# Attention operands of 52 rows without cleared rows, values stored 17 wide, first stack load moved forward

## The chip, the cores and the metric

The kernel runs on one core of a Trainium2 chip (trn2). The metric is the device time of one execution in microseconds; the time of a kernel is the median of several executions. TensorE (PE, with its weight loads as PEld), VectorE (DVE), ScalarE (ACT) and GpSimd (POOL) compute; SyncE (SP) issues nearly all DMAs here, on one hardware queue that 16 DMA engines serve.

## What is computed

Two layers over x of shape (4, 1024, 256), each an attention and a mixture of experts:

```python
x = x + attn_a(layernorm(x)); x = x + ffn(layernorm(x))
x = x + attn_b(layernorm(x)); x = x + ffn(layernorm(x))
# attn_a: S = (K @ Q.T) * 16 ** -0.5 - (i - j), minus infinity where j > i; C = softmax(S); C @ V @ o_w.T + o_b
# attn_b: the usual causal attention, q @ k.T / 4, without the distance term
# 16 heads of 16 channels, T = 1024
# ffn: 2 shared experts (mean) and 32 routed ones, 6 a token by softmax weight; hidden 176, ReLU
```

## The kernel before

A loop over the layers L = 0, 1 has four stages, each closed by phase_end: every engine drains and adds to s_phase, and goes on when all five have done so.

Stage 0, projection. The 4096 tokens are 8 blocks of 512, block n = 2 b + r of batch b and half r. PE (qkv_block, L1507) forms keys, queries and values of a block in six groups; ACT copies each from PSUM with its bias to fqk or vf; DVE (qkv_block, L759) casts fqk to the high part in qkst[:, r] (L766), POOL (qk_lo) subtracts for the low part (L1383, semaphore s_pl). PE transposes the values and DVE copies them from PSUM to vst[:, r] (L776, s_vs): per block two copies of 512 elements a partition. vst is 32 wide for each head: 16 channels and ones set once a layer by a memset (L755). SP's store_block(b, r) (L398) waits for s_pl, sends four stores of 512 KB to qks_scratch (L404, s_pd[r]), waits for s_vs and sends four value stores of 256 KB in runs of 512 bytes to v_scratch (L410, s_vd[r]). DVE waits for s_pd[r] of batch b - 1 before it casts block (b, r), and for s_vd[r] before it copies its values.

The attention works on units: unit u is 4 heads of one batch, 16 units a layer. Its operands are a stack, a [128 rows, 2, 4 heads, 1024] region of SBUF for queries and keys; three stacks r = 0, 1, 2 are used in turn. Rows 0 to 47 are the channels three times over (high by high, high by low, low by high), loaded in six DMAs of 256 KB, 16 rows each (load_stack, L426). Rows 48 to 67 come from rows_scratch (load_rows, L420: two DMAs of 320 KB): zeros, the distance terms, and ones for the rows that bring in the maximum. Line 429 loads rows 66 and 67, 32 KB, after the wait for load_rows. Rows 64 to 127 are cleared first by memsets: DVE L790 and POOL L1392 for stack 0, POOL L1400 and L1407 for stacks 1 and 2. A memset may start when PE has read the xT blocks or POOL and the stores have read qkst, which lie in the same SBUF.

SP's order at the end of stage 0 is: store_block of batches 0 to 2, load_rows(0), load_stack(0, 0), store_block(3, 0), load_rows(1), load_stack(1, 1), store_block(3, 1), phase_end. Within that, load_stack(0, 0) needs the stores of batch 0. PE, after its last transposes, waits for s_vs and for stack 0 (L1722) and then runs the 38 max jobs of unit 0 (max_job, L1545): matmuls of scores into a PSUM bank, a bf16 mask matmul on the diagonal (L1556), and a DVE reduction (L801). DVE gathers the negated maxima, PE transposes them, DVE splits them (L816, L818), and PE ends the stage.

Stage 1, attention. SP waits for all stores of stage 0 (L457, L458), then load_neg_max(0) (L464) writes the negated maxima into rows 66 and 67 of the stack, then load_values(0, 0) (L433), load_rows(2), load_stack(2, 2) and the rest. PE's first_scores(0) waits for the neg-max rows. step(u) then waits for the stack of unit u + 1, whose max jobs it interleaves with the 12 slots of unit u: scores (L1566) with a bf16 mask (L1570) on the diagonal, ACT's exp (L1251), values (L1583). The stationary operand of values is 32 wide, one head for each 32 columns of PE, and the 17th column gives the denominator. Line 1722 stands in stage 0; the matmuls of L1552 and L1566 read all 128 rows of the stack.

Stage 2 runs the shared experts and the routing, stage 3 the routed experts. Neither is touched.

## Time and profile before

| | us |
|---|---|
| median of 3 runs (3132.0 to 3141.73) | 3137.55 |
| profiled execution | 3133.94 |
| its span | 3132.1 |
| granted TensorE clock, mean | 0.928 |
| PE busy, DVE busy, ACT busy, POOL busy | 2618.7, 2071.9, 1640.4, 1413.3 |
| layer 1: last value copy of stage 0 ends | 109.86 |
| layer 1: first max job; first score | 122.74; 160.49 |
| layer 2: first max job; first score | 1678.27; 1716.40 |

Times inside an execution are microseconds from the first instruction of the span. The page gives busy time and shares, the chain of work that ended last, and the costliest groups of instructions; the trace answers for single stretches, lines and DMAs. "Idle before" is what the engine waited before an instruction and for whom. SPq is the sequencer of SP, which issues the DMAs.

### The profile page before, as it was taken

What the parts mean: (1) busy time and instruction counts of PE and PEld (TensorE: products, weight loads), DVE (VectorE), ACT (ScalarE), POOL (GpSimd) and SP (SyncE); (2) the same over time, 40 slices, a digit from 0 to 9 for tenths busy, and PEclk for the clock granted to TensorE, in tenths of its full rate; (3) what the DMA queues carried; (4) which work ended last, traced back from release to release, by engine and by line L of the source; (5) the groups of instructions that cost most, each with busy time, mean ns of one, the idle gap of its engine ahead of it and who ended that gap; (6) DMA issues with size and microseconds to landing.
All of it is one profiled execution on the core that took longest, in us unless ns stands there. A gap on an engine that the chain in (4) does not pass through costs nothing.

```text
span 3132.1 us, 72446 instructions
## 1 busy us (share of the span) xinstructions
PE 2618.7 (84%) x17832; PEld 1949.9 (62%) x17832; DVE 2071.9 (66%) x4604; ACT 1640.4 (52%) x2861; POOL 1413.3 (45%) x1058
## 2 busy tenths in 40 slices
PE   7699999999882899999285999999998819999882
PEld 6455565556562888888273555555555618888882
DVE  8666676676551788777395666766775517777772
ACT  3145444544421788888341554444444208888882
POOL 3430002314155688888544200032232557888885
PEclk9899999999986999999697999999999859999996
DMA  6975655555655799888759743565457558998888
GB/s 223 231 164 124 144 100 112 146 121 165 223 192 184 158 157 154 154 153 154 172 190 208 137 84 80 100 156 117 118 157 238 201 182 147 158 157 150 151 150 204
DMA packets 317281, 494.55 MB, mean 158 GB/s; under 512 B 55706, under 2 KB 225052, under 8 KB 311772
## 3 DMA queue, kind: packets, MB, share of 16 engines
q1 hardware_dynamic: 224908, 361.85, 44.1%
q0 software_dynamic: 92160, 130.08, 24.6%
q8 instruction: 106, 1.74, 0.2%
q14 instruction: 107, 0.88, 0.1%
HBM read 264.26 MB, written 256.77 MB: 166 GB/s over the span
## 4 chain that ended last, share of the span: by engine, by line
PE 47%; DMA 16%; issue 16%; POOL 6%; DVE 6%; SPq 3%; DVEq 2%; POOLq 2%; ACT 2%; ACTq 1%
PE ps L1566 11%; PE ps L1552 11%; PE ps L1583 10%; DMA expert_sum<-x,route_u 7%; DMA expert_rows<-x 4%; PE ps L1833 4%; POOL expert_rows L1433 3%; PE ps L1570 2%; PE ps L1851 2%; POOL expert_sum L1467 2%; PE ps L1556 2%; DMA expert_rows<-work,x 2%; SPq L410 2%; PE ps L1628 1%; DMA split<-rows_scratch 1%
## 5 line engine op out<-in xcount | busy, mean ns | idle before, releaser
L1251 ACT ACTIVATE work<-ps 128x1024 f32<-128x1024 f32 (+3 forms) x768 | 594.5, 810 | 663.8 <-PE ps L1570 436.3
L1467 POOL DMA_INDIRECT expert_sum<-x,route_u x512 | 832.0, 1625 | 194.6 <-issue 102.3
L801 DVE TENSOR_REDUCE small<-ps 128x1 f32<-128x512 f32 (+3 forms) x1216 | 726.7, 655 | 211.6 <-PE ps L1556 140.1
L1433 POOL DMA_INDIRECT expert_rows<-x x288 | 284.6, 988 | 1123.5 <-DVE x L957 722.6
L1552 PE MATMUL ps<-split 128*128 128x512 f32 (+3 forms) x1536 | 511.5, 409 | 66.8 <-DVE work L829 35.3
L1566 PE MATMUL ps<-split 128*128 128x512 f32 (+3 forms) x1536 | 499.4, 405 | 28.1 <-DMA split<-split 27.1
L1833 PE MATMUL ps<-split 128*88 128x256 f32 x3072 | 418.0, 285 | 88.1 <-DVE split L1140 61.2
L1833 PEld LDWEIGHTS ps<-split 128*88 128x88 f32 x3072 | 363.9, 156 | 139.3 <-issue 138.4
L1552 PEld LDWEIGHTS ps<-split 128*128 128x128 f32 x1536 | 277.2, 201 | 262.2 <-DVE small L801 137.9
L1851 PE MATMUL ps<-split 97*128 97x256 f32 x3072 | 408.8, 282 | 2.0 <-DVE split L1155 2.0
L1851 PEld LDWEIGHTS ps<-split 97*128 97x128 f32 x3072 | 384.7, 189 | 2.4 <-issue 2.4
L1566 PEld LDWEIGHTS ps<-split 128*128 128x128 f32 x1536 | 299.0, 201 | 87.1 <-ACT work L1251 39.9
L1583 PE MATMUL ps<-work,split 128*32 128x512 f32 (+3 forms) x3072 | 329.9, 504 | 2.6 <-issue 2.6
L1821 PE MATMUL ps<-ident,x 128*128 128x128 f32 x1024 | 156.8, 276 | 115.7 <-DMA osb<-in_b1r 115.6
L1329 ACT ACTIVATE split<-split 97x512 fp32r x256 | 161.5, 631 | 162.7 <-issue 148.1
L1124 DVE CAST split<-work 128x352 fp32r x256 | 101.7, 397 | 217.0 <-issue 158.1
L1315 ACT ACTIVATE x<-ps,osb 88x256 f32<-88x256 f32 x512 | 228.8, 471 | 30.6 <-issue 15.1
L1570 PE MATMUL ps<-maskk,identb 128*128 128x128 bf16 x1024 | 233.3, 235 | 0.0
L1341 ACT ACTIVATE x<-ps,osb 128x256 f32<-128x256 f32 x512 | 212.4, 465 | 25.9 <-DMA expert_sum<-x,route_u 17.0
L1821 PEld LDWEIGHTS ps<-ident,x 128*128 128x128 f32 x1024 | 120.6, 143 | 116.7 <-issue 116.6
L1148 DVE TENSOR_TENSOR split<-split 97x512 fp32r<-97x512 f32 x256 | 176.2, 688 | 21.5 <-issue 9.2
L1556 PE MATMUL ps<-maskq,identb 128*128 128x128 bf16 (+2 forms) x704 | 187.1, 266 | 0.0
(179 smaller groups left out, 3255.6 us busy)
## 6 DMA issues: line engine op xcount, KB each, us to landing
x<-expert_rows SPq DMA_DIRECT2D x256, 320.0 KB
split<-qks_scratch SPq DMA_DIRECT2D x192, 256.0 KB
qks_scratch<-split SPq DMA_DIRECT2D x64, 512.0 KB, 4.5
expert_rows<-in_pads SPq DMA_DIRECT2D x65, 320.0 KB, 15.8
v_scratch<-work SPq DMA_DIRECT2D x64, 256.0 KB, 4.3
split<-v_scratch SPq DMA_DIRECT2D x32, 512.0 KB, 14.4
xT_scratch<-split SPq DMA_DIRECT2D x16, 1024.0 KB
split<-xT_scratch SPq DMA_DIRECT2D x16, 1024.0 KB
```

The source lines that it names most:

```text
L801: v.tensor_reduce(cols[:, heads[0]:heads[0] + len(heads), i], ps[:, task_bank(n), 0:w * len(heads)].rearrange("p (h k) -> p h k", k=w), AX ...
L1251: c.activation(pexp[:, (s % 2) * 2 + h, :, BLK - w:], ps[:, 2 * h:2 * h + 2, BLK - w:], ACT.Exp).then_inc(s_pe, 1)
L1433: pool.indirect_dma_start(rows, bass.IndirectOffsetOnAxis(ap=posu[b][:, t * 8 + k:t * 8 + k + 1], axis=0), rowb[b][:, t // TPB, t % TPB, : ...
L1467: pool.indirect_dma_start(acc[r], bass.IndirectOffsetOnAxis(ap=idx[:, j, k:k + 1], axis=0), ye[:, r3, k, :], None, compute_op=ALU.add).the ...
L1552: last = mm(bank[:, e, :], stack[:, r, 0, h, i * P:i * P + P], stack[:, r, 1, h, first:first + w], start=e == 0, stop=not diagonal and e = ...
L1556: last = mm(bank[:, :, w - P:w], identb[:, :], maskq[:, :].unsqueeze(1).broadcast_to([P, len(heads), P]), start=False, stop=True, skip_gro ...
L1566: last = mm(ps[:, h, BLK - w:], stack[:, r, 1, h, kb * P:kb * P + P], stack[:, r, 0, h, (qt + 1) * BLK - w:(qt + 1) * BLK], start=True, st ...
L1570: last = mm(ps[:, h, BLK - w:BLK - w + P], identb[:, :], maskk[:, :], start=False, stop=True, skip_group_check=True)
L1583: last = mm(ps[32 * h:32 * h + 32, 6, BLK - w:], vreg[:, r, kb, h, :], pexp[:, (s % 2) * 2 + h // 2, h % 2, BLK - w:], start=kb == 0, stop ...
L1821: last = tr(ps[:, r, k * TT + n * P:k * TT + n * P + P], xrow[:, r3, n, k * P:k * P + P], ident[:, :])
L1833: last = mm(ps[0:HC, 2 + c, 0:TT], w1e[:, r, ws, k * HID + c * HC:k * HID + c * HC + HC], xe[:, r, xp, k * TT:k * TT + TT], start=e == 0 a ...
L1851: last = mm(ps[:, 4 + 2 * (j % 2) + n, 0:D], he[0:HB, r, xp, c * TT + n * P:c * TT + n * P + P], w2e[0:HB, r3, ws, c * D:c * D + D], start ...
```

## The change

SROWS goes from 68 to 52. Rows 48 and 49 are the distance terms, 50 and 51 the maximum; no zeros are left, and the score and max matmuls read rows 0 to 51 of the stack. All memsets of stack rows go, with their waits, and load_rows waits for PE's projections instead, of blocks 0 to 3 for stack 0 and of all blocks for the others. POOL's last batch joins its loop. Values are 17 wide in SBUF and DRAM, and one DMA moves a unit's four tiles as one run of 1088 bytes a partition; DVE's copy becomes four, one for each unit. SP's loop stops a batch earlier: load_rows(0) comes ahead of batch 2's stores, load_stack(0, 0) between its two, and both stores of batch 3 ahead of load_rows(1) and load_stack(1, 1). load_neg_max(0) comes ahead of the wait for the stores.

```diff
@@ -66,7 +66,8 @@
 HG = 4
 NU = B * H // HG
 NQB = T // P
-SROWS = 68
+SROWS = 52
+VW = HD + 1
 
 NPHASE = 4
 ENGINES = 5
@@ -163,7 +164,7 @@
 
 def build(nc, a, out):
     qks = nc.dram_tensor("qks_scratch", (2, 2, NU, 64, T), F32, kind="Internal").ap()
-    vds = nc.dram_tensor("v_scratch", (NU, P, NQB, HG * 32), F32, kind="Internal").ap()
+    vds = nc.dram_tensor("v_scratch", (NU, P, 2, TPB * HG * VW), F32, kind="Internal").ap()
 
     xd = nc.dram_tensor("x_scratch", (NTOK, D), F32, kind="Internal").ap()
     xtd = nc.dram_tensor("xT_scratch", (NBLK, P, XB), F32, kind="Internal").ap()
@@ -191,7 +192,7 @@
 
         stack = split[:, 0:24576].rearrange("p (r o h t) -> p r o h t", r=3, o=2, h=HG)
         stack32 = stack.bitcast(F32)
-        vreg = split[:, 24576:27648].bitcast(F32).rearrange("p (r t h c) -> p r t h c", r=3, t=NQB, h=HG)
+        vreg = split[:, 24576:24576 + 3 * NQB * HG * VW].bitcast(F32).rearrange("p (r t h c) -> p r t h c", r=3, t=NQB, h=HG)
         wqkv = wreg[:, 0:3072].rearrange("p (m k s n) -> p m k s n", m=3, k=KD, s=2)
         qkst = wreg[:, 3072:11264].rearrange("p (r m s f t) -> p r m s f t", r=2, m=2, s=2, f=2)
         xs = split[:, 16384:20480].rearrange("p (r k s t) -> p r k s t", r=2, k=KD, s=2)
@@ -236,7 +237,7 @@
         pexp = work[:, 8192:12288].rearrange("p (r h t) -> p r h t", r=4, h=2)
         xn = work[:, 8192:10240].rearrange("p (r t d) -> p r t d", r=2, t=TPB)
         fqk = work[:, 0:2048].rearrange("p (r f t) -> p r f t", r=2, f=2)
-        vst = work[:, 2048:6144].rearrange("p (r t h c) -> p r t h c", r=2, t=TPB, h=H)
+        vst = work[:, 2048:2048 + 2 * TPB * H * VW].rearrange("p (r u t h c) -> p r u t h c", r=2, u=HG, t=TPB, h=HG)
         vf = work[:, 6144:8192].rearrange("p (r f t) -> p r f t", r=2, f=2)
         mask32 = work[:, 0:4 * P].rearrange("p (m k) -> p m k", m=4)
         rwraw = work[:, 512:576].rearrange("p (k e) -> p k e", k=KD)
@@ -300,8 +301,6 @@
         s_ph, s_pl, s_pd = sem("qk_hi_done"), sem("qk_lo_done"), [sem(f"qk_stored{r}") for r in range(2)]
         s_vt, s_vs, s_vd = sem("v_transposed"), sem("v_staged"), [sem(f"v_stored{r}") for r in range(2)]
         s_rows = [sem(f"constant_rows_loaded{r}") for r in range(3)]
-        s_zero = [sem(f"stack_zeroed{r}") for r in range(3)]
-        s_zq = sem("first_query_stack_zeroed")
         s_vl = [sem(f"values_loaded{r}") for r in range(3)]
         s_stk = [sem(f"stack_loaded{r}") for r in range(3)]
         s_st, s_pe, s_pv = sem("scoresT_ready"), sem("exp_done"), sem("values_done")
@@ -408,14 +407,13 @@
                     sp.wait_ge(s_vs, n + 1 + 1)
                     for u in range(HG):
                         sp.dma_start(
-                            vds[b * HG + u, :, r * TPB:(r + 1) * TPB, :],
-                            vst[:, r, :, HG * u:HG * u + HG, :].rearrange("p t h c -> p t (h c)")
+                            vds[b * HG + u, :, r, :],
+                            vst[:, r, u].rearrange("p t h c -> p (t h c)")
                         ).then_inc(s_vd[r], 16)
 
                 def load_rows(r):
-                    sp.wait_ge(s_zero[r], (L + 1) * (1 if r == 0 else 2))
-                    if r == 0:
-                        sp.wait_ge(s_zq, L + 1)
+                    sp.wait_ge(s_pj, (L * NBLK + (4 if r == 0 else NBLK)) * 6)
+                    apart(sp)
                     for o in range(2):
                         sp.dma_start(stack32[48:SROWS, r, o], rows_scratch[L, o].unsqueeze(1)
                                      .broadcast_to([SROWS - 48, HG, T])).then_inc(s_rows[r], 16)
@@ -426,18 +424,18 @@
                             sp.dma_start(stack32[16 * g:16 * g + 16, r, o],
                                          qks[o, s, u].rearrange("(h w) t -> w h t", h=HG)).then_inc(s_stk[r], 16)
                     sp.wait_ge(s_rows[r], (L + 1) * 32)
-                    sp.dma_start(stack32[66:68, r, 0], rows_scratch[L, 0, 0:2].unsqueeze(1)
+                    sp.dma_start(stack32[SROWS - 2:SROWS, r, 0], rows_scratch[L, 0, 2:4].unsqueeze(1)
                                  .broadcast_to([2, HG, T])).then_inc(s_stk[r], 16)
 
                 def load_values(u, r):
-                    sp.dma_start(vreg[:, r], vds[u].rearrange("p t (h c) -> p t h c", h=HG)).then_inc(s_vl[r], 16)
+                    sp.dma_start(vreg[:, r], vds[u].rearrange("p r (t h c) -> p (r t) h c", t=TPB, h=HG)).then_inc(s_vl[r], 16)
 
                 def load_unit(u, r):
                     sp.wait_ge(s_pv, (L * NU + u - 2) * NS + 2)
                     load_stack(u, r)
                     load_values(u, r)
 
-                with sp.Fori(0, B - 1) as b:
+                with sp.Fori(0, B - 2) as b:
                     for r in range(2):
                         store_block(b, r)
 
@@ -445,23 +443,22 @@
                 load_rows(0)
                 for r in range(2):
                     sp.wait_ge(s_pd[r], (L * B + 1) * 64 + 64)
+                store_block(B - 2, 0)
                 load_stack(0, 0)
-                store_block(B - 1, 0)
+                store_block(B - 2, 1)
+                for r in range(2):
+                    store_block(B - 1, r)
                 load_rows(1)
                 load_stack(1, 1)
-                store_block(B - 1, 1)
                 phase_end(sp, L, 0)
 
 
-                for r in range(2):
-                    sp.wait_ge(s_pd[r], (L * B + B) * 64 + 64)
-                    sp.wait_ge(s_vd[r], (L * B + B) * 64 + 64)
                 TASKS = L * LAYER_TASKS
 
                 def load_neg_max(u):
                     sp.wait_ge(s_mr, TASKS + max_task(u) + 1 + 3)
                     for s in range(2):
-                        sp.dma_start(stack32[66 + s:67 + s, u % 3, 0].rearrange("p h t -> p (h t)"),
+                        sp.dma_start(stack32[SROWS - 2 + s:SROWS - 1 + s, u % 3, 0].rearrange("p h t -> p (h t)"),
                                      mhl[:, s, :].bitcast(F32)).then_inc(s_mrow, 16)
 
                 def load_x_blocks(b):
@@ -497,6 +494,9 @@
                     sp.dma_start(xs[:, r].rearrange("p k s t -> p (k s t)").bitcast(F32), xtd[blk]).then_inc(s_xsl[r], 16)
 
                 load_neg_max(0)
+                for r in range(2):
+                    sp.wait_ge(s_pd[r], (L * B + B) * 64 + 64)
+                    sp.wait_ge(s_vd[r], (L * B + B) * 64 + 64)
                 load_values(0, 0)
                 load_rows(2)
                 load_stack(2, 2)
@@ -752,7 +752,7 @@
                 x_lo(0, 0)
                 x_lo(1, 1)
                 input_var(1)
-                v.memset(vst[:, :, :, :, HD:32], 1.0)
+                v.memset(vst.rearrange("p r u t h c -> p (r u t h) c")[:, :, HD:VW], 1.0)
                 input_scales(1)
                 normalise_block(2, 0)
 
@@ -772,9 +772,10 @@
                         x_lo(blk + 2, r)
                     dve.wait_ge(s_vd[r], (L * B + b) * 64 + 64)
                     dve.wait_ge(s_vt, n + 1 + 2)
-                    for f in range(2):
-                        last = v.tensor_copy(vst[:, r, :, 8 * f:8 * f + 8, 0:HD],
-                                             ps[:, 6 + f, :].rearrange("p (t h c) -> p t h c", t=TPB, h=8))
+                    for u in range(HG):
+                        last = v.tensor_copy(vst[:, r, u, :, :, 0:HD],
+                                             ps[:, 6 + u // 2, :].rearrange("p (t h c) -> p t h c", t=TPB, h=8)
+                                             [:, :, u % 2 * HG:u % 2 * HG + HG, :])
                     last.then_inc(s_vs, 1)
                     if r == 0 and b < B - 2:
                         input_var(b + 2)
@@ -786,8 +787,6 @@
                     qkv_block(B - 2, r, 3 - r)
 
 
-                dve.wait_ge(s_pj, (L * NBLK + 4) * 6)
-                v.memset(stack32[64:P, 0, 0], 0.0).then_inc(s_zq, 1)
                 for r in range(2):
                     qkv_block(B - 1, r, 1 - r)
 
@@ -1383,30 +1382,12 @@
                             p.tensor_tensor(qkst[:, r, m, 1, f], fqk[:, m, f], qkst[:, r, m, 0, f].bitcast(F32),
                                             ALU.subtract).then_inc(s_pl, 1)
 
-                with pool.Fori(0, B - 1) as b:
+                with pool.Fori(0, B) as b:
                     for r in range(2):
                         qk_lo(b, r)
-                pool.wait_ge(s_pj, (L * NBLK + 4) * 6)
-                pool.wait_ge(s_pl, (L * NBLK + 6) * 4 + 4)
-                apart(pool)
-                p.memset(stack32[64:P, 0, 1], 0.0).then_inc(s_zero[0], 1)
-                pool.wait_ge(s_zero[0], L + 1)
-                for r in range(2):
-                    qk_lo(B - 1, r)
-                pool.wait_ge(s_pj, (L + 1) * (NBLK * 6))
-                pool.wait_ge(s_pl, (L + 1) * (NBLK * 4) + 4)
-                apart(pool)
-                for o in range(2):
-                    p.memset(stack32[64:P, 1, o], 0.0).then_inc(s_zero[1], 1)
                 phase_end(pool, L, 0)
 
-                for s in range(2):
-                    pool.wait_ge(s_pd[s], (L * B + B) * 64 + 64)
-                apart(pool)
-                for o in range(2):
-                    p.memset(stack32[64:P, 2, o], 0.0).then_inc(s_zero[2], 1)
                 pool.wait_ge(s_bo, L * 16 + 16)
-                pool.wait_ge(s_zero[2], (L + 1) * 2)
                 apart(pool)
                 with pool.Fori(0, NT) as t:
                     xt = x[:, ds(t * D, D)]
@@ -1549,8 +1530,8 @@
                     diagonal = first + w == (i + 1) * P
                     task_free(n)
                     for e, h in enumerate(heads):
-                        last = mm(bank[:, e, :], stack[:, r, 0, h, i * P:i * P + P],
-                                  stack[:, r, 1, h, first:first + w], start=e == 0,
+                        last = mm(bank[:, e, :], stack[0:SROWS, r, 0, h, i * P:i * P + P],
+                                  stack[0:SROWS, r, 1, h, first:first + w], start=e == 0,
                                   stop=not diagonal and e == len(heads) - 1, skip_group_check=True)
                     if diagonal:
                         last = mm(bank[:, :, w - P:w], identb[:, :],
@@ -1563,8 +1544,8 @@
                     pe.wait_ge(s_pe, (U * NS + s) * 2 + half + 1)
                     for e in range(2):
                         h = 2 * half + e
-                        last = mm(ps[:, h, BLK - w:], stack[:, r, 1, h, kb * P:kb * P + P],
-                                  stack[:, r, 0, h, (qt + 1) * BLK - w:(qt + 1) * BLK],
+                        last = mm(ps[:, h, BLK - w:], stack[0:SROWS, r, 1, h, kb * P:kb * P + P],
+                                  stack[0:SROWS, r, 0, h, (qt + 1) * BLK - w:(qt + 1) * BLK],
                                   start=True, stop=kb < 4 * qt, skip_group_check=True)
                         if kb >= 4 * qt:
                             last = mm(ps[:, h, BLK - w:BLK - w + P], identb[:, :], maskk[:, :], start=False, stop=True,
@@ -1580,7 +1561,7 @@
                         pe.wait_ge(s_vl[r], (L * (6, 5, 5)[r] + u // 3 + 1) * 16)
                     pe.wait_ge(s_pe, (U * NS + s) * 2 + 2 + 2)
                     for h in range(HG):
-                        last = mm(ps[32 * h:32 * h + 32, 6, BLK - w:], vreg[:, r, kb, h, :],
+                        last = mm(ps[32 * h:32 * h + VW, 6, BLK - w:], vreg[:, r, kb, h, :],
                                   pexp[:, (s % 2) * 2 + h // 2, h % 2, BLK - w:], start=kb == 0,
                                   stop=kb == 4 * qt + 3, skip_group_check=True)
                     last.then_inc(s_pv, 1)
@@ -1925,9 +1906,9 @@
     r["zeros"] = np.zeros((P, D), f)
     t = np.arange(T, dtype=f)
     rows = np.zeros((NL, 2, SROWS - 48, T), f)
-    rows[0, 0, 16], rows[0, 0, 17] = -t, 1.0
-    rows[0, 1, 16], rows[0, 1, 17] = 1.0, t
-    rows[:, 1, 18:20] = 1.0
+    rows[0, 0, 0], rows[0, 0, 1] = -t, 1.0
+    rows[0, 1, 0], rows[0, 1, 1] = 1.0, t
+    rows[:, 1, 2:4] = 1.0
     r["rows"] = rows
     r["ident"] = np.eye(P, dtype=f)
     q, k = np.arange(P)[:, None], np.arange(P)[None, :]
```

## Rows read from the trace of the kernel before

**Rows 1.** The page's first lines: span, busy time and share of each engine.

```profile
span 3132.1 us, 72446 instructions
...
PE 2618.7 (84%) x17832; PEld 1949.9 (62%) x17832; DVE 2071.9 (66%) x4604; ACT 1640.4 (52%) x2861; POOL 1413.3 (45%) x1058
```

**Rows 2.** Windows of layer 1: busy us (count) per engine, PEclk, DMA share, GB/s.

```profile
108.60:122.70 14.10, 0.00 (x0) 0.00 (x0) 1.26 (x2) 0.00 (x0) 6.01 (x2) 0.54 1.02 187
...
147.80:160.50 12.70, 0.01 (x1) 0.02 (x1) 0.00 (x0) 1.28 (x1) 5.97 (x2) 0.50 0.55 186
160.50:1184.00 1023.50, 904.15 (x6016) 611.09 (x6017) 654.50 (x1484) 490.34 (x764) 344.69 (x311) 0.93 0.63 153
```

**Rows 3.** Chain that ended last, layer 1's stage change: start us, us, what.

```profile
100.96 9.88 DMA split<-rows_scratch
...
127.69 11.40 DMA split<-rows_scratch
...
151.10 6.32 DMA v_scratch<-work
157.58 0.59 SPq L464
158.22 2.13 DMA split<-split
```

**Rows 4.** Timeline, same stretch: start us, us, engine, line, tiles [idle before <-releaser].

```profile
108.57 1.29 DVE L776 COPY work<-ps 128x512 f32<-128x512 f32 x2 [3.43 <-PE ps L1527]
...
122.74 1.11 PE L1552 MATMUL ps<-split 128*128 128x128 f32 x4 [14.21 <-DMA split<-rows_scratch]
...
147.42 0.28 DVE L818 TENSOR_TENSOR split<-ps,split 32x128 fp32r<-32x128 f32 x1
...
160.49 0.79 PE L1566 MATMUL ps<-split 128*128 128x512 f32 x1 [13.42 <-DMA split<-split]
```

**Rows 5.** Line 404's stores: issued 82.5 to 84.5, then 111.2 to 113.0.

```profile
DMA to landing us min/median/max: 2.8/4.1/5.0
...
L404 SPq DMA_DIRECT2D qks_scratch<-split x4: 410/562/820, 111.2 to 113.0; - x4
...
DMA to landing us min/median/max: 10.2/12.1/14.5
```

**Rows 6.** Windows while stacks load and while stores run, columns as in group 2.

```profile
104.00:116.00 12.00, 3.68 (x20) 2.67 (x18) 2.42 (x4) 2.06 (x3) 10.10 (x5) 0.73 1.03 130
118.00:124.00 6.00, 1.26 (x6) 1.27 (x6) 0.00 (x0) 0.00 (x0) 0.00 (x0) 0.50 1.03 308
```

**Rows 7.** Timeline of DVE and POOL in the projection stage.

```profile
25.66 1.76 DVE L755 MEMSET work<- 128x2048 f32 x1 [0.38 <-issue]
...
84.64 3.59 DVE L766 CAST split<-work 128x512 fp32r<-128x512 f32 x4
...
95.63 5.49 POOL L1383 TENSOR_TENSOR split<-work,split 128x512 fp32r<-128x512 f32 x4 [1.31 <-DVE split L766]
```

**Rows 8.** Timeline of PE in unit 2: scores, mask, values.

```profile
267.39 0.23 PE L1570 MATMUL ps<-maskk,identb 128*128 128x128 bf16 x1
...
267.43 0.48 PE L1566 MATMUL ps<-split 128*128 128x512 f32 x1
...
267.75 0.23 PE L1570 MATMUL ps<-maskk,identb 128*128 128x128 bf16 x1
...
267.91 1.07 PE L1583 MATMUL ps<-work,split 128*32 128x512 f32 x8
```

**Rows 9.** The page's costliest groups: the mask matmuls.

```profile
L1570 PE MATMUL ps<-maskk,identb 128*128 128x128 bf16 x1024 | 233.3, 235 | 0.0
...
L1556 PE MATMUL ps<-maskq,identb 128*128 128x128 bf16 (+2 forms) x704 | 187.1, 266 | 0.0
```

**Rows 10.** Timeline of layer 2: first job and first score.

```profile
1678.27 1.11 PE L1552 MATMUL ps<-split 128*128 128x128 f32 x4 [13.24 <-DMA split<-rows_scratch]
...
1716.40 0.79 PE L1566 MATMUL ps<-split 128*128 128x512 f32 x1 [13.71 <-DMA split<-split]
```

## The prediction

> **What bounds the kernel now.** I read the page first: TensorE is busy 84% of the span, more than any other engine [rows 1]. Then the windows of layer 1. From 160.5 us on, through all sixteen units of the attention stage, PE is busy 904 of 1023 us at a granted clock of 0.93, while the DMA engines are busy 63% [rows 2]. There only something that makes PE itself faster or slower counts, or an earlier start of the whole stage. Between the last projection (108.6) and the first score (160.49) it is the other way round: PE and DVE stand still in 108.6 to 122.7 and again in 147.8 to 160.5, with the clock near its lower level, and in the first of the two the DMA share is 1.02 [rows 2]. The chain of waits in time says what they stand still for: the rows load of stack 0 (9.88 us), then, after PE's jobs, the rows load of stack 1 (11.40), the last value store (6.32), and the row of negated maxima (issued at 157.58, landed 2.13 us after its issue) [rows 3]. The timeline gives the two ends: PE's first max job at 122.74 is released by line 429's rows load after 14.21 us of idling, though the value copy it also needs is over at 108.57 + 1.29 = 109.86; DVE ends the maxima at 147.42 + 0.28 = 147.70; the first score starts at 160.49 [rows 4]. Layer 2 has the same two points at 1678.27 and 1716.40 [rows 10]: 38.1 us apart, 37.75 in layer 1. So I take one layer and double it.
>
> **The stack load, moved forward and made smaller.** Before, the rows load can't be issued until both memsets and every store of batch 2 have gone by, at 99.85. Now it is issued after batch 1's stores, about 79, on four partitions in place of twenty, and landed long before the stack is wanted. The six loads of stack 0 and line 429's go out behind store_block(2, 0), whose qk stores were issued up to 84.5 and landed within 5.0 us [rows 5]; its value stores follow, so the queue reaches the stack at about 90 (88 to 92). From the end of the rows load (100.96 + 9.88 = 110.84) to PE's release (122.74) the same seven loads took 11.9 us [rows 3, 4]. That gives 102, or up to 3 more where the rows load (a fifth of the bytes, half the 4 KB pieces on each of the engines that carry it) still lies ahead. The loads are slow whatever stands beside them: 130 GB/s with a DMA share of 1.03 in 104 to 116, against 308 GB/s when stores run in 118 to 124 [rows 6]. So 12 us of this queue are shifted, not saved.
>
> **What is behind them in the queue.** store_block(2, 1) is now issued at 91 behind the stack. Its qk stores hold the staging half r = 1, and DVE may not cast the last block before they have landed. Before, the stores issued behind the stack landed 10.2 to 14.5 us after issue, the last at 113.0 + 14.5 = 127.5, 4.8 us after the stack's last row [rows 4, 5]. So they land now at 102 + 4.8 = 107 (105 to 112), where DVE would have wanted them at 100.6. That is the new wait. Queued behind it on DVE are four casts (3.59 us when nothing holds them up [rows 7]) and the value copy, which releases PE. The copy is now four of 256 elements for two of 512 (1.29 us for both [rows 4]): at least 1.29, at most 2.58 if each costs what a long one does; I take 1.5. 107 + 3.6 + 1.5 = 112, plus 1 for the later landing of the value stores that the copy also waits for: the first max job starts at **113** (110 to 119) in place of 122.74.
>
> **To the first score.** The max jobs took 147.70 - 122.74 = 25.0 us, set by DVE's reductions, which don't change: 138. SP must also be through. POOL's four subtractions (5.49 us [rows 7]) end at about 113, so the last qk stores go out by 116 and the last value stores by 118; the queue works off two blocks of 2.5 MB at 308 GB/s, 8.2 us each, from 108: to 124.7. rows(1) takes up to 9.88 / 2 = 4.9 us, stack 1 another 11.9: 141.5. SP itself is past the barrier at about 132, as the wait for the rows is its last. The neg-max rows are issued at 138.3, 2.9 us ahead of a first score when the queue is empty (157.58 to 160.49 [rows 3, 4]), and behind the stack's tail otherwise. First score at **142.5** (139.5 to 150), 18 us sooner. The wait for s_pd and s_vd, which ended 9.9 us after the maxima and was ahead of the neg-max rows (157.58 against 147.70 [rows 3, 4]), now stands behind them, when both are met. load_values(0, 0) has 8 us before its first use, and moves 272 KB for 512. Stack 1 is wanted at once after the first scores and lands at 141.5: met, by a hair. If it is 5 us late, those 5 us are in the upper bound.
>
> **Small parts.** The memset of the ones writes 128 elements for 2048: some 1.6 of its 1.76 us go from DVE at 25.66 [rows 7], where DVE is never idle; of this I count 1.6 less 0.2 to 0.3 for each of the first blocks' longer value copies, 0.5 us a layer (-0.5 to 1.5). POOL's and DVE's memsets of 3.5 to 7 us lie beside PE's projections or the waits already counted: nothing more. Value stores and loads move 17/32 of the bytes in runs of 1088 for 512 bytes: nothing, as stores in the projection stage land in 2.8 to 5.0 us and are not waited for [rows 5]; during the attention stage the queue has a third of its time free. If the queue had no such room the narrower value would be a gain.
>
> **The matmuls themselves.** Scores and max jobs now have 52 rows instead of 128, at the same columns; values have 17 stationary columns for 32. No matmul of this trace has 64 rows or fewer, so this is bounded by neighbours. Below nothing: a mask is followed by values 0.16 us later, by a score 0.04 us later (267.75 to 267.91, 267.39 to 267.43 [rows 8]), so a value group carries 0.12 us that could shrink with its weights; 12 slots by 32 units are 384 groups, -46 us at the very most. Above: see the second rival. I take nought, since the moving columns stay and the score with its mask has a period of 0.36 us, 267.39 to 267.75 [rows 8], of which 640 columns at 2.4 GHz are 0.27.
>
> **The sum.** 2 x (18 + 0.5) = 37 us. The profiled execution took 3133.94 us around its span of 3132.1; 3133.9 - 37 = 3097. The median of the runs is 3.6 above it: 3100.5. Rounded **3100**, with 2 x 11 to 2 x 21 us for the bounds of this case: 3095 to 3116.
>
> **Rivals.** *Start not moved.* The stack ahead of store_block(2, 1) costs the last block all it gains: DVE's casts then end so late that the max jobs begin at 122.7 as before. Only the tail gains: 147.7 + 0.3 (my estimate for the barrier, as above) + 2.9 = 150.9 for 160.5, 19 us in two layers, 3118. For it: the stores took 14.5 us behind a stack [rows 5]; against: the queue is 10 us ahead.
>
> *Slower: the row count changes how PE is divided.* In this trace a change from the full array to 32 columns (mask to values) costs 0.12 us more than mask to score, which stay in one form [rows 8]. If 52 rows is a form of its own, every mask (1024 + 704 = 1728 of them [rows 9], 128 rows each) forces a change in and out, in a stage that PE bounds. At 0.12 each that is 207 us: 3100 + 207 = 3307. It decides from 37 / 1728 = 0.021 us a mask. Against it: there is already a gap of 0.36 - 0.27 = 0.09 us around each mask that may hide one of the two. The Trainium skill (TensorEngine Tiling (Array Packing), Key Properties) lists 64 rows by 128 columns as a tiling mode of its own and says that changing mode drains the engine; the 0.12 us at the change of columns agrees with it, and for rows no run here shows it.
>
> *Nothing changes by over 0.3%.* Another transfer, stack 1 above all, ends as late as the old chain: 3137.
>
> *PE gains too.* Half of the 46 us: 3077.
>
> **Chances.** Forecast 0.56, start not moved 0.10, change of form 0.24 (0.20 with over 0.027 us a mask, which is slower than before by over 0.3%; 0.02 within, 0.02 still faster), no change 0.04, PE gains 0.06. About 0.3%, 9.4 us, is what a measurement can tell from nothing. Faster 0.56 + 0.10 + 0.02 + 0.06 = 0.74; same 0.04 + 0.02 = 0.06; slower 0.20. The range reaches down to 3085, which leaves out most of PE's gain (0.04), and up to 3190, 0.052 us a mask (1728 x 0.052 = 90), which leaves out some 0.14.
>
> **What would show it.** First max job near 113 and first score near 142.5 in both layers; DVE's cast of the last block waiting for a qk store until 107; the seven stack loads still slow; the time from first score to the stage's end unchanged within 3 us. The prediction is wrong if a score and its mask take other than 0.36 us, if value groups take other than 1.00 us, or if PE waits for stack 1 after the first scores.

## The result, and the profile after

| | before | after |
|---|---|---|
| median, us | 3137.89 (4 runs, 3132.0 to 3141.73) | 4400.0 (4 runs, 4386.9 to 4402.18) |
| span of the profiled execution, us | 3132.1 | 4385.1 |
| granted TensorE clock, mean | 0.928 | 0.669 |
| forecast, us | | 3100 (3085 to 3190) |

The changed kernel takes 1.4016 times as long, 95% interval 1.3988 to 1.4044: 1262 us more, where 37 us less were forecast. The forecast is wrong in sign, and the change is over thirty times as large as forecast.

In the changed kernel the lines around the attention stand lower: the max jobs are L1533 (L1552 before) and their mask L1537 (L1556), the scores L1547 (L1566) and their mask L1551 (L1570), the values L1564 (L1583). The page of the changed kernel, its first lines, the row of the granted clock in 40 slices (tenths) and its groups of PE:

```profile
span 4385.1 us, 72388 instructions
...
PE 3955.8 (90%) x17832; PEld 2432.5 (55%) x17832; DVE 2130.8 (49%) x4634; ACT 1673.1 (38%) x2861; POOL 1368.4 (31%) x1048
...
PEclk9555555565555679999785555555655556799997
...
L1547 PE MATMUL ps<-split 52*128 52x512 f32 (+3 forms) x1536 | 900.0, 620 | 7.4 <-DMA split<-split 7.4
...
L1533 PE MATMUL ps<-split 52*128 52x512 f32 (+3 forms) x1536 | 826.7, 610 | 33.5 <-DVE work L828 18.8
...
L1564 PE MATMUL ps<-work,split 128*17 128x512 f32 (+3 forms) x3072 | 554.7, 820 | 0.0
...
L1551 PE MATMUL ps<-maskk,identb 128*128 128x128 bf16 x1024 | 287.9, 281 | 0.0
```

The same three groups of the kernel before:

```profile
L1552 PE MATMUL ps<-split 128*128 128x512 f32 (+3 forms) x1536 | 511.5, 409 | 66.8 <-DVE work L829 35.3
L1566 PE MATMUL ps<-split 128*128 128x512 f32 (+3 forms) x1536 | 499.4, 405 | 28.1 <-DMA split<-split 27.1
...
L1583 PE MATMUL ps<-work,split 128*32 128x512 f32 (+3 forms) x3072 | 329.9, 504 | 2.6 <-issue 2.6
```

PE waits no more than it did: its idle time ahead of these groups has shrunk (66.8 to 33.5, 28.1 to 7.4), the count of matmuls is the same 17832, and it is busy 3955.8 us against 2618.7 [rows 1]. The same instructions simply take longer. The scores went from a mean of 405 to 620 ns; the value matmuls, which stream the same columns as before, from 504 to 820 (means over all their forms). The row of the clock says where: 5 (half rate) with one 6 through both attention stages, and mostly 9 elsewhere.

Windows of the changed kernel (busy us and count for PE, PEld, DVE, ACT and POOL; granted clock, DMA share, GB/s), the columns of [rows 2], where 160.5 to 1184 had 0.93. The second ends with the last value matmul of layer 1's attention (1457.8):

```profile
170.00:1200.00 1030.00, 1022.11 (x3402) 486.17 (x3402) 388.55 (x774) 261.78 (x330) 66.07 (x69) 0.52 0.28 64
170.00:1458.00 1288.00, 1277.07 (x4307) 608.03 (x4306) 477.92 (x974) 333.90 (x422) 96.84 (x102) 0.53 0.28 67
```

The attention of layer 1 in the kernel before, whose last value matmul starts at 831.0:

```profile
170.00:831.00 661.00, 636.43 (x4313) 377.24 (x4317) 449.76 (x977) 319.32 (x423) 111.31 (x123) 0.98 0.57 139
```

The stage is nearly twice as long. From the first score to the last value matmul it takes 1457.8 - 149.97 = 1307.8 us for 831.0 - 160.49 = 670.5, and in layer 2 3646.0 - 2330.0 = 1316.0 for 2386.9 - 1716.4 = 670.5. Together these are 1283 us more, so the whole loss lies there. PE is busy 1277 of 1288 us at a granted clock of 0.53, where it was busy 636 of 661 at 0.98: it runs at the lower of its two levels (1.2 GHz) nearly all the time although the profile shows almost no idle time on it. It stays there: in 611 to 617, with PE busy without a gap, the clock is 0.50, where the kernel before has 1.00 in 612 to 617.

The timeline of PE in that stretch (start us, us, engine, line, tiles), a value group and two scores, each with its mask:

```profile
612.20 1.91 PE L1564 MATMUL ps<-work,split 128*17 128x512 f32 x8
614.04 0.79 PE L1533 MATMUL ps<-split 52*128 52x512 f32 x1
614.76 0.29 PE L1537 MATMUL ps<-maskq,identb 128*128 128x128 bf16 x1
614.98 0.79 PE L1533 MATMUL ps<-split 52*128 52x512 f32 x1
615.70 0.29 PE L1537 MATMUL ps<-maskq,identb 128*128 128x128 bf16 x1
```

A score with its mask takes 614.98 - 614.04 = 0.94 us (0.36 in [rows 8]), a value group 614.04 - 612.20 = 1.84 (1.00 before). The lower clock alone doesn't make 0.94. The kernel before also has moments at the lower level, just after its first score, and there the pair takes 161.17 - 160.49 = 0.68:

```profile
160.49 0.79 PE L1566 MATMUL ps<-split 128*128 128x512 f32 x1 [13.42 <-DMA split<-split]
161.08 0.33 PE L1570 MATMUL ps<-maskk,identb 128*128 128x128 bf16 x1
161.17 0.78 PE L1566 MATMUL ps<-split 128*128 128x512 f32 x1
```

Score to mask was 0.59 and is 0.72, mask to score was 0.09 and is 0.22: 0.13 us more at each of the two changes between 52 and 128 rows, 0.26 a pair. So there are two suspects, a lower clock and a change of form.

The stage change itself went nearly as forecast. The timeline of layer 1:

```profile
109.17 3.56 DVE L766 CAST split<-work 128x512 fp32r<-128x512 f32 x4 [10.41 <-DMA qks_scratch<-split]
112.65 1.41 DVE L776 COPY work<-ps 128x256 f32<-128x256 f32 x4
...
146.64 0.28 DVE L817 TENSOR_TENSOR split<-ps,split 32x128 fp32r<-32x128 f32 x1
```

DVE does wait for a qk store of store_block(2, 1), until 109.17 (107 forecast); the chain of waits has that store as its longest piece of this stretch, 93.12 to 109.05. The first max job starts at 114.30 (113 forecast; 122.74 in [rows 4]) and the first score at 149.97 (142.5 forecast; 160.49). Between the two the max jobs take 146.92 - 114.30 = 32.6 us instead of 25.0: here too PE is slow, with a clock of 0.52 in 108 to 150 (0.72 before) and a change of rows on both sides of each mask.

### The profile page after: what moved, and what is told of

It reads as the page before. It is cut to its first block, busy times and chain, and to the rows that moved or that the text cites. A ratio compares the mean times of both kernels' runs of the same rounds, so it can differ in the third digit from the quotient of the medians.

```text
span 4385.1 us, 72388 instructions
## 1 busy us (share of the span) xinstructions
PE 3955.8 (90%) x17832; PEld 2432.5 (55%) x17832; DVE 2130.8 (49%) x4634; ACT 1673.1 (38%) x2861; POOL 1368.4 (31%) x1048
## 4 chain that ended last, share of the span: by engine, by line
PE 66%; issue 11%; DMA 9%; POOL 4%; DVE 4%; DVEq 2%; SPq 1%; POOLq 1%; ACT 1%; ACTq 0%
PE ps L1547 18%; PE ps L1533 16%; PE ps L1564 12%; PE ps L1551 5%; PE ps L1537 4%; DMA expert_sum<-x,route_u 4%; PE ps L1814 3%; DMA expert_rows<-x 2%; PE ps L1832 2%; POOL expert_rows L1414 2%; DMA expert_rows<-work,x 2%; PE ps L1631 1%; POOL expert_sum L1448 1%; DVE split L1139 1%; PE ps L1574 1%
## 5 line engine op out<-in xcount | busy, mean ns | idle before, releaser
L1250 ACT ACTIVATE work<-ps 128x1024 f32<-128x1024 f32 (+3 forms) x768 | 621.2, 810 | 1885.4 <-PE ps L1551 1289.1
L800 DVE TENSOR_REDUCE small<-ps 128x1 f32<-128x512 f32 (+3 forms) x1216 | 783.0, 661 | 931.2 <-PE ps L1537 642.2
L1547 PE MATMUL ps<-split 52*128 52x512 f32 (+3 forms) x1536 | 900.0, 620 | 7.4 <-DMA split<-split 7.4
L1533 PE MATMUL ps<-split 52*128 52x512 f32 (+3 forms) x1536 | 826.7, 610 | 33.5 <-DVE work L828 18.8
L1533 PEld LDWEIGHTS ps<-split 52*128 52x128 f32 x1536 | 419.9, 305 | 440.4 <-issue 258.2
L1547 PEld LDWEIGHTS ps<-split 52*128 52x128 f32 x1536 | 437.4, 292 | 251.9 <-ACT work L1250 80.3
L1564 PE MATMUL ps<-work,split 128*17 128x512 f32 (+3 forms) x3072 | 554.7, 820 | 0.0
L1551 PE MATMUL ps<-maskk,identb 128*128 128x128 bf16 x1024 | 287.9, 281 | 0.0
L1551 PEld LDWEIGHTS ps<-maskk,identb 128*128 128x128 bf16 x1024 | 105.8, 103 | 285.2 <-issue 263.1
L1537 PE MATMUL ps<-maskq,identb 128*128 128x128 bf16 (+2 forms) x704 | 234.1, 332 | 0.0
L1537 PEld LDWEIGHTS ps<-maskq,identb 128*128 128x128 bf16 x704 | 73.0, 104 | 257.0 <-issue 248.6
```

What stands on the lines that cost most here:

```text
L800: v.tensor_reduce(cols[:, heads[0]:heads[0] + len(heads), i], ps[:, task_bank(n), 0:w * len(heads)].rearrange("p (h k) -> p h k", k=w), AX ...
L1250: c.activation(pexp[:, (s % 2) * 2 + h, :, BLK - w:], ps[:, 2 * h:2 * h + 2, BLK - w:], ACT.Exp).then_inc(s_pe, 1)
L1533: last = mm(bank[:, e, :], stack[0:SROWS, r, 0, h, i * P:i * P + P], stack[0:SROWS, r, 1, h, first:first + w], start=e == 0, stop=not diag ...
L1537: last = mm(bank[:, :, w - P:w], identb[:, :], maskq[:, :].unsqueeze(1).broadcast_to([P, len(heads), P]), start=False, stop=True, skip_gro ...
L1547: last = mm(ps[:, h, BLK - w:], stack[0:SROWS, r, 1, h, kb * P:kb * P + P], stack[0:SROWS, r, 0, h, (qt + 1) * BLK - w:(qt + 1) * BLK], st ...
L1551: last = mm(ps[:, h, BLK - w:BLK - w + P], identb[:, :], maskk[:, :], start=False, stop=True, skip_group_check=True)
```

## The experiments

Theory A: what counts is the number of rows that the score and max matmuls read. With fewer, the granted clock goes down, whatever the rows hold. Theory B: it is the pauses in PE at each change between 52 and 128 rows that keep the clock down. Theory C: a change of form also costs time of its own. Theory D: the narrower values, the copies or the new order of transfers have a part in it. The texts put down ahead of the first four runs use other letters for two things: "A64" is the theory that only a matmul of 64 rows or fewer is another form of the array, and "C" is the 17 columns of the values, a part of D here.

### Only fewer rows read, in the kernel before

```
-  stack[:, r, 0, h, ...], stack[:, r, 1, h, ...]
+  stack[0:SROWS, r, 0, h, ...], stack[0:SROWS, r, 1, h, ...]     # SROWS = 68, max jobs and scores
```

Rows 68 to 127 of a stack are zeros in the kernel before, so this leaves out only multiplications by zero.

> The kernel before, with one edit: its score and max matmuls read rows 0 to 67 of the stack instead of all 128 (rows 68 on are zeros, so nothing else changes). Theory A, fewer rows of the array in use, whatever their number, keep the granted clock down: slower, by 200 us and more, clock in the attention stage below 0.9. Theory A64, only a matmul of 64 rows or fewer is another form of the array: no difference, 3138 within 10 us, score and mask 0.36 us apart. Theory C, the 17 columns of the values are to blame: no difference either.

3633.04 us (3612.37 to 3652.86), ratio 1.1601 (1.1549 to 1.1653). The row of the clock, and a window of layer 1:

```profile
PEclk9679655655668799999785896665565686999996
...
170.00:1200.00 1030.00, 988.47 (x4763) 585.36 (x4763) 535.00 (x1171) 354.29 (x464) 166.60 (x180) 0.69 0.45 114
```

The clock falls to 0.69 in this stretch, from 0.94 in the same window of the kernel before, and the kernel takes 496 us more, with the same instructions, the same columns, the same loads and stores. A mask at 613 us and the max matmul behind it: 68 rows are of the same form as 128 (mask to score 0.09 us at the lower clock, as before):

```profile
613.30 0.33 PE L1556 MATMUL ps<-maskq,identb 128*128 128x128 bf16 x1
613.39 0.67 PE L1552 MATMUL ps<-split 68*128 68x384 f32 x1
```

That is theory A, with no change of form in it. A64 had forecast no difference, so a change of form can't be all of it.

### The change with 68 rows

```
-SROWS = 52
+SROWS = 68
-    rows[:, 1, 2:4] = 1.0
+    rows[:, 1, SROWS - 50:SROWS - 48] = 1.0
```

> The changed kernel with SROWS back at 68 and still no cleared rows: rows 52 to 65 are zeros loaded from DRAM, the matmuls read rows 0 to 67. Everything else of the change stays. Theory A: slow as the first run of this set, less the gain of the new order. Theory A64: clock 0.93 again, first max job at 115 to 120 (the rows loads are 320 KB again), first score at 143 to 148, 3138 less 25 to 35 us: 3103 to 3113. Theory C: still above 4000.

3625.86 us (3600.13 to 3642.59), ratio 1.1575 (1.1532 to 1.1618). The window, then a score and its mask at the upper clock:

```profile
170.00:1200.00 1030.00, 979.80 (x4745) 577.47 (x4745) 530.52 (x1166) 353.69 (x462) 169.28 (x175) 0.70 0.43 112
```

```profile
310.33 0.47 PE L1547 MATMUL ps<-split 68*128 68x512 f32 x1
310.65 0.23 PE L1551 MATMUL ps<-maskk,identb 128*128 128x128 bf16 x1
310.69 0.47 PE L1547 MATMUL ps<-split 68*128 68x512 f32 x1
```

The pair takes 0.36 us, as in [rows 8]: at the upper level, 68 rows cost nothing. A64's 3103 to 3113 fails here too. Everything else of the change is in this kernel, and it stands within the noise of the first experiment; the 36 us that this rest turns out to gain further down can't be seen beside the 40 us between the runs of either. So 488 of the 1262 us are there with 68 rows, and 774 (4400 - 3626) come with going from 68 to 52.

### Only the narrower values

```
-  ps[32 * h:32 * h + 32, 6, ...], vreg[:, r, kb, h, :]
+  ps[32 * h:32 * h + 17, 6, ...], vreg[:, r, kb, h, 0:17]      # in the kernel before
```

> The kernel before, with only the stationary operand of the value matmuls cut from 32 to 17 columns (storage unchanged). Theories A and A64: 3138 within 10 us, a value group of 512 columns still takes 1.00 us. Theory C, 17 columns of each 32 keep the clock down: above 3700, granted clock near 0.67.

3140.4 us in one run, against 3137.35 (3132.54 to 3144.31, 7 runs) for the kernel before, clock 0.93 in 170 to 1200. In that run the 17 columns neither cost nor bring anything that could be told from the spread of the kernel before.

### The masks in halves of 64 rows

The changed kernel, with each mask matmul of 128 rows split into two of 64, so that a score and its mask have the same form:

```
-  mm(..., identb[:, :], maskk[:, :], start=False, stop=True)
+  for z, (idn, msk) in enumerate(((identb[0:64, :], maskk[0:64, :]), (identh, maskkh))):
+      mm(..., idn, msk, start=False, stop=z == 1)               # the same for maskq
```

> The changed kernel, with each mask matmul of 128 rows split into two of 64 rows on the same half of the array as the scores, so that score and mask never differ in rows. 52 rows and 17 columns stay. Theory A64, clock part from the rows: the granted clock stays at 0.5 in the attention stage, score and mask period falls from 0.94 to 0.75 to 0.80 us, the whole to 4050 to 4200. Theory B, the clock is down because the changes of form leave pauses on PE: clock back at 0.9 and more, 3150 to 3300. Theory C: clock at 0.5 as well, so this run tells B from the others.

4156.41 us in one run. Its window, and one score with its two half masks:

```profile
170.00:1200.00 1030.00, 1019.32 (x4419) 572.68 (x4415) 422.93 (x846) 285.76 (x360) 92.55 (x96) 0.53 0.31 74
```

```profile
613.10 0.77 PE L1540 MATMUL ps<-split 52*128 52x512 f32 x1
613.68 0.33 PE L1545 MATMUL ps<-maskq,identb 64*128 64x128 bf16 x1
613.80 0.31 PE L1545 MATMUL ps<-halfb 64*128 64x128 bf16 x1
613.88 0.77 PE L1540 MATMUL ps<-split 52*128 52x512 f32 x1
```

With 1728 matmuls more it is 244 us faster, and both the time (4050 to 4200) and the period (0.75 to 0.80) are those forecast. The score goes over to its mask after 0.58 us, not 0.72, and the whole period is 0.78 in place of 0.94; 1728 x 0.16 = 276 us would be the gain if all were like this one. The second half mask costs 613.80 - 613.68 = 0.12, 1728 x 0.12 = 207: without it the changes of form at the masks would be worth some 244 + 207 = 450 us, against 1728 x 0.26 = 449 by the pair. But the clock stays at 0.53, with almost no pauses left at the masks. Theory B falls as the main cause, theory C holds. A small part of the pauses in the low clock isn't excluded: the masks read 64 rows here, and 0.53 is so near 0.50, the lower level, that little could show.

### All of the change, with 128 rows read

This puts back what the change removed from the operands, and keeps the rest. The stacks have 64 rows of data, rows 64 to 127 are cleared as before, and the matmuls read all 128. The order of loads and stores, the four-fold value copies and the 17-wide values are those of the change.

```
-SROWS = 52
+SROWS = 64                                  # rows[:, 1, SROWS - 50:SROWS - 48] = 1.0
+    ...                                     # semaphores s_zero, with waits on PE, VectorE and GpSimd
+    v.memset(stack32[64:P, 0, o], 0.0)      # VectorE, between the last two projection blocks
+    p.memset(stack32[64:P, 1, o], 0.0)      # GpSimd, end of stage 0; the same for stack 2, a stage later
-  stack[0:SROWS, r, ...]
+  stack[:, r, ...]                          # max jobs and scores
```

> The changed kernel with its own order of loads and stores, its 17-wide values and its four-fold value casts, but score and max matmuls that read all 128 rows, of which 64 to 127 are cleared again (operands of 64 rows, the clearing on VectorE for stack 0 and on GpSimd for stacks 1 and 2). All of the work is computed. Theory A (what was lost lies only in the number of rows the matmuls read; the earlier start of the attention is worth what was forecast): the granted clock is back at 0.93 in 170:1200, the first max job stands near 114 us and the first score near 142 to 146 us, and the time is 3100 to 3115 us against 3137 of the kernel before. Theory D (the new order of transfers or the casts cost something of their own, hidden so far beneath the slow matmuls): the clock is back but the time is 3137 or above.

3099.88 us (3094.13 to 3105.22, 5 runs) against 3135.57 (3132.51 to 3146.66, 13 runs): ratio 0.988 (0.9859 to 0.9902), 36 us faster than the kernel before, 1.2%, with an interval that leaves out nought. Theory A had forecast 3100 to 3115. Its page and window:

```profile
span 3092.3 us, 72412 instructions
...
PEclk9899999999986999999698999999999859999996
```

```profile
170.00:1200.00 1030.00, 905.41 (x6094) 618.60 (x6090) 663.43 (x1509) 505.14 (x805) 342.86 (x294) 0.94 0.62 150
```

Its timeline at the two stage changes (the max jobs are L1548 here, the scores L1562):

```profile
109.32 3.56 DVE L767 CAST split<-work 128x512 fp32r<-128x512 f32 x4 [1.92 <-DMA qks_scratch<-split]
...
112.81 1.41 DVE L777 COPY work<-ps 128x256 f32<-128x256 f32 x4
...
114.55 1.11 PE L1548 MATMUL ps<-split 128*128 128x128 f32 x4 [7.12 <-DVE work L777]
...
139.37 0.28 DVE L821 TENSOR_TENSOR split<-ps,split 32x128 fp32r<-32x128 f32 x1
...
145.23 0.79 PE L1562 MATMUL ps<-split 128*128 128x512 f32 x1 [6.22 <-DMA split<-split]
...
1677.80 0.79 PE L1562 MATMUL ps<-split 128*128 128x512 f32 x1 [4.46 <-DMA split<-split]
```

The first score is 160.49 - 145.23 = 15.3 us sooner in layer 1, and 1716.40 - 1677.80 = 38.6 sooner in layer 2 [rows 4, 10]; the span is 39.8 shorter. Theory D (the transfers or the copies cost something of their own) falls. This version beats both kernels.

### How the clock depends on the rows

The kernel before, with max jobs and scores that read `stack[0:96, ...]`, and with `stack[0:112, ...]`; the rest of the rows is zeros.

> The kernel before with score and max matmuls that read 96 of the 128 rows (the rest is zeros, so nothing of the result is left out). If the granted clock falls with the number of rows gradually, the time lies between 3137 us (128 rows, clock 0.93 in 170:1200) and 3633 us (68 rows, 0.69), around 3300 to 3450. If there is one step between 68 and 128 rows, it is equal to one of the two ends.

> The kernel before with score and max matmuls that read 112 of the 128 rows (the rest is zeros, nothing of the result is left out). With a gradual dependence the time lies between that of 96 rows and 3137 us; with a step above 112 rows it is near 3633 us; with one below 96 it is 3137 us.

96 rows: 3230.54 us (3211.78 to 3249.29), ratio 1.0295 (1.0233 to 1.0357). 112 rows: 3152.4 us (3138.91 to 3162.98), ratio 1.004 (1.0016 to 1.0065). In 170 to 1200 the clock is 0.87 and 0.93.

That window isn't the same work in every kernel. The last value matmul of layer 1 starts at 831.0 us in the kernel before, at 1080.4 in the first experiment and at 1457.8 in the changed kernel. So in the faster kernels 170 to 1200 also holds later work, stages 2 and 3 above all, which the change doesn't touch (831 to 1200 in the kernel before: clock 0.87). The attention stage alone, from 170 us to its last value matmul, for 112, 96 and 68 rows in the kernel before, then for 64 rows in the changed one (the run of the next section):

```profile
170.00:842.00 672.00, 645.49 (x4321) 382.59 (x4318) 451.61 (x977) 318.94 (x423) 110.55 (x122) 0.96 0.57 137
170.00:893.00 723.00, 697.81 (x4329) 411.31 (x4329) 455.43 (x978) 321.32 (x424) 111.14 (x123) 0.88 0.53 128
170.00:1080.00 910.00, 891.48 (x4319) 506.85 (x4318) 466.80 (x978) 327.52 (x424) 111.04 (x123) 0.66 0.42 102
170.00:1455.00 1285.00, 1274.09 (x4307) 605.57 (x4306) 477.43 (x974) 334.44 (x422) 97.21 (x102) 0.53 0.28 68
```

There is no single step between 128 and 68: 128, 112, 96 and 68 rows give a clock of 0.98, 0.96, 0.88 and 0.66 in the attention, and 3137, 3152, 3231 and 3633 us. Both forecasts of a gradual fall held in sign; 96 rows lie below the 3300 to 3450 that I had named, since the loss is small at first.

### 64 rows

The changed kernel with `SROWS = 64` (and the two ones of `rows` moved along).

> The changed kernel with operands of 64 rows in place of 52 (nothing left out). 52 and 64 rows differ from 68 in that they fit in half of the array. If the form is what counts below 68 rows, this is like 52 rows: 4300 to 4450 us, the pair of a 512-wide score and its mask at 0.94 us and a clock of 0.50 to 0.57 in 170:1200. If only the number of rows counted, it would be close to the 3626 us of 68 rows, 3650 to 3750.

4378.97 us (4373.44 to 4384.49), ratio 1.3955 (1.3911 to 1.3998). PE at 613.95:

```profile
613.95 0.79 PE L1533 MATMUL ps<-split 64*128 64x512 f32 x1
614.68 0.29 PE L1537 MATMUL ps<-maskq,identb 128*128 128x128 bf16 x1
614.90 0.79 PE L1533 MATMUL ps<-split 64*128 64x512 f32 x1
```

The pair takes 0.95 us and the clock is 0.53 in 170 to 1200. Twelve more rows than 52 bring 21 us; four more, from 64 to 68, bring 753. The change of form begins between 64 and 68 rows.

### The change of form where the clock is high

The masks in halves of 64 rows again, now in the kernel before with its 128-row scores: the form changes at each mask and back.

> The kernel before (score and max matmuls of 128 rows, values 32 wide), with each mask matmul of 128 rows split into two of 64 rows: 1728 matmuls more, and a change of form from 128 to 64 rows and back around each mask pair. Nothing is left out. It measures the change of form where the granted clock is high. Theory C (a change of form costs time of its own, 0.27 us for the two of a pair at the lower clock, so 0.13 us at the upper one): a pair of a 512-wide score and its mask takes 0.36 + 0.13 + some 0.07 for the second half, about 0.56 us, and the time is 1728 x 0.2 = some 350 us above 3137 us, 3350 to 3550, with the granted clock in 170:1200 still at 0.85 or more. Rival (a change of form costs nothing, the 0.27 us in the changed kernel came with the low clock alone): the pair takes 0.36 + 0.07 = 0.43 us, and the time is 3200 to 3280 us.

3848.7 us (3830.01 to 3867.4), ratio 1.2274 (1.213 to 1.2418). The window, then a stretch in which the clock is 1.00:

```profile
170.00:1200.00 1030.00, 1006.61 (x5208) 500.20 (x5208) 474.30 (x1003) 332.23 (x428) 121.51 (x137) 0.81 0.39 92
```

```profile
218.73 0.49 PE L1574 MATMUL ps<-split 128*128 128x512 f32 x1
219.16 0.23 PE L1579 MATMUL ps<-maskk,identb 64*128 64x128 bf16 x1
219.22 0.22 PE L1579 MATMUL ps<-halfb 64*128 64x128 bf16 x1
219.37 0.50 PE L1574 MATMUL ps<-split 128*128 128x512 f32 x1
```

The period is 0.64 us for 0.36 [rows 8]. Score to mask is 0.43 for 0.32, the second half 0.06, mask to score 0.15 for 0.04: 0.11 at each change, 0.22 a pair. So a change of form costs nearly as much at the upper clock as the 0.13 at the lower one, and I had expected half. By the pair the kernel would lose 1728 x 0.28 = 484 us; it loses 713, and the clock of the stretch is 0.81 where I had expected 0.85 or more (and 0.56 us for the pair, 3350 to 3550 for the kernel). The remaining 229 us are put down to the clock, which fell from 0.98 to 0.81 in the attention (170 to 1190 here); that is a difference, not a measurement. Whether it is the 64 rows of the masks or the pauses beside them that lower it here wasn't told apart.

## Why the prediction was wrong

**What bounds the kernel: right.** PE sets the attention stage, and only what makes PE faster or slower counts. That made the error dear: PE is busy 1337 us more (3955.8 less 2618.7), and the kernel takes 1262 us more. One reading of [rows 2] was off: 160.5 to 1184 isn't the attention stage alone, whose last value matmul starts at 831.0; the rest is later work, at a clock of 0.86. In the attention itself PE was busy 636 of 661 us at 0.98, so PE bounded it more tightly than 904 of 1023 says, and there was more clock to lose than 0.93 shows.

**The stack load and the queue behind it: right, to some 2 us.** The stack's loads go out at 88.3 in both versions (88 to 92 forecast), DVE's wait ends at 109.2 to 109.3 (107), the value copy takes 1.41 us (1.5), the first max job starts at 114.3 and 114.55 (113). The four value copies of 256 elements cost 0.12 more than the two of 512 [rows 4].

**To the first score: right with 128 rows, with one term short.** The max jobs take 139.65 - 114.55 = 25.1 us (25.0). The row of negated maxima is issued at 139.79, and the score starts 5.4 us later, not 2.9 as in [rows 3, 4]: the second of its two transfers takes 4.66 us for 2.13. Stack 1 isn't what it waits behind, since the DMA share has fallen to 0.22 in 140 to 142; what holds it up isn't shown. That gives 145.2 for 142.5, inside 139.5 to 150. In layer 2 it is 1677.80 - 1642.25 = 35.6 us from the last transposes of the values to the first score for 1716.40 - 1663.94 = 52.5 before, 16.9 saved for 18. "Start not moved" falls with it, and so does "nothing changes".

**The matmuls themselves: this step failed, twice.** "I take nought, since the moving columns stay" was argued from columns and clock cycles. Neither of the two things that fewer rows change is a cycle of a matmul.

*First, the granted clock.* It was in none of the rivals, though I had read 0.93 in [rows 2] and took it as given. With 68 rows a matmul costs the same at the upper level (0.36 us a pair), but PE is at that level for less of the time: clock 0.98 to 0.66 in the attention, and 3137 to 3633 us in the kernel before, 3100 to 3626 in the changed one. The sum needed a term for it, about 500 us for 60 rows less, and no row that the prediction shows could size it. The Trainium skill (TensorE: Matmul & The Clock Gate, What's actually happening) describes the gate as one that follows how busy PE is; here PE is busy 1277 of 1288 us at a clock of 0.53 and was busy 636 of 661 at 0.98, so busy time alone doesn't tell it.

*Second, the change of form.* It was there as the second rival, at 0.24, with the right place and the right count of 1728, but mis-sized: "at 0.12 each" for each mask, taken from the gap at a change of columns. It is 0.11 to 0.13 at each change and a mask has two, so 0.22 to 0.26 us a mask. The 0.09 us gap that was to hide one of the two hides nothing. At 0.26 that is 450 us, where the rival had 207; the halved masks bear it out with 244 + 207. The rule that the rival took from the Trainium skill (TensorEngine Tiling (Array Packing), Key Properties), that changing the tiling mode drains the engine, agrees with this: the step is between 64 and 68 rows. (The list of modes that it named with it stands on that page under Available Configurations.) The prediction had said that it would be wrong if a score and its mask took other than 0.36 us, and that is the sign that came, 0.94.

**The account.** From 3100 us (128 rows read) to 4400: 526 with 68 rows, where only the clock of the attention was seen to change (0.97 to 0.67); 753 from 68 to 64, of which some 450 are the changes of form and the remaining 300 go with the clock (0.67 to 0.53); 21 from 64 to 52. The three are differences of whole kernels. The split of the 753 is worked out, not measured, and whether its 300 come from the four rows, from the pauses or from the form itself stays open. So does the reason why fewer rows lower the clock at all; shown is that reading fewer of them does it.

**Small parts: right.** 17 columns for 32 are worth nothing that shows (3140.4 in one run against 3137.35). "PE gains too", which had 23 us from them, falls: in the version with 128 rows the 1536 value matmuls of layer 1 are busy 161.9 us for 165.2. From the first score of layer 1 to the last transposes of the values in layer 2 that version takes 1642.25 - 145.23 = 1497.0 us for 1663.94 - 160.49 = 1503.5. These 6.4 us are more than the 0.5 that I counted for the memset, and less than the spread of the kernel's own runs; where they come from stays open. With them the gain of the spans closes: 15.3 + 6.4 + 16.9 are 38.6 of the 39.8.

**The sum of the rest** was 37 us; with the operands read at full height it is 36 (3099.88 against 3135.57), where the text had 3100. The forecast was that of a change without its main part. That the two sums agree to 1 us is in part luck: the first scores gained 2.7 and 1.1 us less than the 18 of the sum, and the 6.4 us, whose origin is open, stand where 0.5 was counted.

## What to carry to other kernels

Rows of an operand that held zeros weren't waste on TensorE here: before trimming the contraction of matmuls that fill a stage, ask what the granted clock will do, and read all 128 rows unless a run shows that it stays. Here 112 rows cost 0.4%, 96 rows 3% and 68 rows 16%. Where trimming goes to 64 rows or fewer beside matmuls of 128, count the changes between the two and take some 0.12 us for each. And when a stage is bound by one engine, a term "the same columns, so nothing" needs a run or a wide range.

## What the runs showed of the hardware that I had not expected

- The granted clock follows the number of rows that the score and max matmuls read, with PE busy 96 to 99% of the attention and even where the rows added are zeros: 0.98, 0.96, 0.88 and 0.66 for 128, 112, 96 and 68 rows, and 0.53 for 64 and for 52, in the attention of layer 1. The last two have the changes of form as well.
- With 52 rows PE stays at 1.2 GHz in a stretch without any gap (611 to 617 us, clock 0.50), so an engine that shows as full is no sign of a high clock.
- A change between 64 rows or fewer and 128 costs 0.11 us at the upper clock and 0.13 at the lower: almost no dependence on the clock. It is no idle time of PE in any view. Its size shows in the distance between starts, and the weight loads have more idle time ahead of them, put down to "issue": 130.4 us at the masks of L1551 in the attention of layer 1, for 24.0 at L1570 before.
